# Weight sums in earlier slots, a shorter wait for one low part, three banks for the down products

## The reference

```
def ffn(x, w_gate, w_up, w_down):          # w_gate, w_up 512 x 2048, w_down 2048 x 512
    h = silu(x @ w_gate) * (x @ w_up)
    g = h.reshape(B, S, 2048 // 4, 4)
    _, idx = top_k(abs(g), 2)              # keep 2 of every 4
    return (g * mask(idx)).reshape(h.shape) @ w_down
x = x + layernorm(attn(layernorm(x)))
x = x + layernorm(ffn(layernorm(x)))
```

## Time and profile before

| | |
|---|---|
| median of 3 runs | 1237.51 us (1236.67 to 1240.82) |
| profiled execution, its own time | 1238.83 us |
| its span in the trace | 1237.0 us |
| mean granted TensorE clock | 0.978 |
| PE busy | 1180.2 us (95%), 5862 matmul records |
| DVE busy | 861.3 us (70%) |
| ACT / POOL busy | 520.7 us (42%) / 504.2 us (41%) |
| DMA | 153.78 MB, mean 124 GB/s |

### The profile page before, as it was taken

The page is one execution under the profiler, slowest core; times in us unless marked ns, Lnnn a source line. Parts: engine busy times, 40 slices in busy tenths (PEclk is TensorE's granted clock), DMA queues, the critical chain, the costliest instruction groups (busy, mean ns, idle before and its releaser), DMA issues.

```text
span 1237.0 us, 16282 instructions
## 1 busy us (share of the span) xinstructions
PE 1180.2 (95%) x5862; PEld 989.3 (80%) x5862; DVE 861.3 (70%) x1416; ACT 520.7 (42%) x1017; POOL 504.2 (41%) x393
## 2 busy tenths in 40 slices
PE   8999999999999999999999899996997899999986
PEld 7888888888888888888888677784885678888865
DVE  8945666666755556666665897967779469768698
ACT  5534535545454345453455333324423244334332
POOL 6422424424644144252455654554523542112124
PEclk9999999999999999999999899996999899999998
DMA  6321423314443233142356467682523555343421
GB/s 217 87 71 43 112 61 89 95 31 119 116 130 90 69 87 95 43 116 52 97 153 204 151 223 249 222 292 79 190 69 102 164 191 181 120 153 119 153 68 69
DMA packets 96368, 153.78 MB, mean 124 GB/s; under 512 B 10272, under 2 KB 31008, under 8 KB 96288
## 3 DMA queue, kind: packets, MB, share of 16 engines
q1 hardware_dynamic: 96288, 152.74, 39.4%
HBM read 96.60 MB, written 40.89 MB: 111 GB/s over the span
## 4 chain that ended last, share of the span: by engine, by line
PE 77%; DVE 13%; DMA 3%; ACT 2%; issue 2%; POOL 2%; SPq 2%; DVEq 0%; ACTq 0%; POOLq 0%
PE bank_q L784 8%; PE bank_q L786 8%; PE bank_q L785 8%; PE bank_y L786 5%; PE bank_y L785 5%; PE bank_y L784 5%; PE bank_od L1011 5%; PE bank_od L1014 4%; PE bank_t L784 3%; PE bank_t L786 3%; PE bank_t L785 3%; PE bank_s L908 2%; PE bank_od L784 2%; PE bank_od L785 2%; PE bank_od L786 2%; PE bank_s L784 2%
## 5 line engine op out<-in xcount | busy, mean ns | idle before, releaser
L784 PE MATMUL bank_q<-x_hi,w_hi 128*128 128x512 f32 x464 | 187.6, 404 | 13.7 <-POOL x_lo L1910 11.6
L786 PE MATMUL bank_q<-x_lo,w_hi 128*128 128x512 f32 x464 | 182.4, 393 | 0.0
L785 PE MATMUL bank_q<-x_hi,w_lo 128*128 128x512 f32 x464 | 182.1, 392 | 0.0
L1910 POOL TENSOR_TENSOR w_lo<-stage,w_hi 128x512 fp32r<-128x512 f32 x60 | 80.5, 1352 | 114.0 <-ACT w_hi L1190 113.2
L1910 POOL TENSOR_TENSOR big_lo<-q_rows,big_hi 128x1024 fp32r<-128x1024 f32 x31 | 73.9, 2385 | 117.1 <-ACT big_hi L1229 117.1
L784 PEld LDWEIGHTS bank_q<-x_hi,w_hi 128*128 128x128 f32 x464 | 88.1, 190 | 31.2 <-POOL x_lo L1910 12.0
L786 PEld LDWEIGHTS bank_q<-x_lo,w_hi 128*128 128x128 f32 x464 | 87.9, 189 | 19.2
L785 PEld LDWEIGHTS bank_q<-x_hi,w_lo 128*128 128x128 f32 x464 | 88.2, 190 | 16.8
L786 PE MATMUL bank_y<-wout_lo,a_hi 128*128 128x512 f32 x256 | 100.0, 391 | 0.0
L785 PE MATMUL bank_y<-wout_hi,a_lo 128*128 128x512 f32 x256 | 99.8, 390 | 0.0
L784 PE MATMUL bank_y<-wout_hi,a_hi 128*128 128x512 f32 x256 | 99.8, 390 | 0.0
(11 more groups left out here) (421 smaller groups left out, 3104.3 us busy)
## 6 DMA issues: line engine op xcount, KB each, us to landing
q_rows<-scratch SPq DMA_DIRECT2D x116, 128.0 KB, 2.3
x_rows<-x SPq DMA_DIRECT2D x48, 256.0 KB, 3.0
stage<-wq SPq DMA_DIRECT2D x32, 256.0 KB, 2.7
stage<-wo SPq DMA_DIRECT2D x32, 256.0 KB, 2.7
s_keep<-x_hi SPq DMA_DIRECT2D x16, 512.0 KB, 4.4
s_keep<-x_lo SPq DMA_DIRECT2D x16, 512.0 KB, 5.3
w_hi<-s_keep SPq DMA_DIRECT2D x32, 256.0 KB, 3.1
w_lo<-s_keep SPq DMA_DIRECT2D x32, 256.0 KB, 3.7
```

The source lines that it names most:

```text
L784: pe.matmul(ps, whi, xhi, start=first, stop=False, skip_group_check=True)
L785: pe.matmul(ps, wlo, xhi, start=False, stop=False, skip_group_check=True)
L786: return pe.matmul(ps, whi, xlo, start=False, stop=last, skip_group_check=True)
L1910: return pool.tensor_tensor(dst, full, hi.bitcast(F32), ALU.subtract)
```

## The change

Seven edits:

1. `t_low(2)`: POOL waits for step 7 of the row sums (counter 8) where it waited for step 8 (counter 9).
2. `SUM_AT`: the 16 rounds are summed in slots 1 to 15, four to a group, where they ran to slot 20, three to a group. A load then stands at most one slot ahead of its sum from round 8 on.
3. Down products of the first block go round three banks (psO, psD, psY) instead of two; the turns (`mid, 1`) all use bank psSt; the addition of a down product is written before the choice.
4. The low part of the last down piece of a unit, made by DVE (L1494), is made by POOL behind the hidden lows; counter dve_wl is gone.
5. DVE's lows of rows 2 and 3 (`first_lows`) come behind the hidden product of the next slot.
6. Down products 29, 30 and 31 are made in slots 36, 38, 40 (before 35, 36, 37); loads and splits of the next unit's last pieces move with them, and `ld_d` has eight semaphores instead of four.
7. Down product 50 is made in slot 64 (before: 61), as one of six; its addition stands between `pair_1` and `keep_masks`, that of 51 between masks and rows.

```diff
-        return y + 6
+        return y + 6 if y < EDGE - 3 else (36, 38, 40)[y - EDGE + 3]
     if y >= LAST:
         return y + 9
-    return SLOTS if y > 50 else 8 * (y // 8) + 11 + min(y % 8, 6)
+    return SLOTS if y > 49 else 8 * (y // 8) + 11 + min(y % 8, 6)
...
+def down_place(y):
+    if y < EDGE:
+        return y % 3
+    return y % 4 if y < SLOTS - 4 else 4 + y % 4
...
-SUM_AT = [1, 2, 3, 5, 6, 7, 9, 10, 11, 13, 14, 15, 17, 18, 19, 20]
+SUM_AT = [1, 2, 2, 3, 5, 6, 6, 7, 9, 10, 10, 11, 13, 14, 14, 15]
...
-DOWN_LD = {NU: (33, 33, 33, 39), NU + 1: (39, 39, 39, 39), NU + 2: (51, 51, 51, 51), NU + 3: (59, 59, 59, 59)}
-DOWN_AT = {NU: (35, 36, 37, 41), NU + 1: (42, 43, 44, 45), NU + 2: (52, 53, 54, 55), NU + 3: (60, 61, 62, 63)}
+DOWN_LD = {NU: (33, 33, 33, 41), NU + 1: (41, 41, 41, 41), NU + 2: (51, 51, 51, 51), NU + 3: (59, 59, 59, 59)}
+DOWN_AT = {NU: (35, 36, 37, 42), NU + 1: (43, 44, 45, 46), NU + 2: (52, 53, 54, 55), NU + 3: (60, 61, 62, 63)}
...
-        psX = [psY, psSt]
+        psX = [psSt, psSt]
...
         def down_bank(y):
-            if y < EDGE:
-                return (psO, psD)[y % 2]
-            if y < SLOTS - 4:
-                return (psO, psD, psY[:, :], psS[:, :])[y % 4]
-            return (gX, uX, gY, uY)[y % 4]
+            return (psO, psD, psY[:, :], psS[:, :], gX, uX, gY, uY)[down_place(y)]
...
-                if y < EDGE + 2:
-                    g.wait_ge(dve_yf, y - 1)
+                g.wait_ge(dve_y, SLOTS)
+                g.wait_ge(dve_yf, same_place(y) + 1)
...
-            def split(k):
-                hi, lo = dest(PLAN[k][0])
-                g.wait_ge(act_wh, k + 1)
-                dve.tensor_tensor(lo, stage[:, k % RING_W, :], hi.bitcast(F32), ALU.subtract).then_inc(dve_wl, 1)
...
+            def first_lows(d):
                 for i in range(2, 4):
                     g.wait_ge(act_hh, 4 * d + i + 1)
                     dve.tensor_tensor(hidden(d)[1][:, i, :], hid[:, i, :], hidden(d)[0][:, i, :].bitcast(F32),
...
-                    keep_two(n // 4 - 1)
                 if n < EDGE:
                     for y in downs:
                         add_down(y)
+                if n % 4 == 0 and 4 <= n <= EDGE:
+                    keep_two(n // 4 - 1)
+                if n == EDGE:
+                    first_lows(n // 4 - 1)
+                if n % 4 == 1 and 4 < n < EDGE:
+                    first_lows(n // 4 - 1)
...
                     keep_masks(NU - 1, 0)
+                    add_down(downs[1])
                     keep_rows(NU - 1, 0)
                     hidden_lows(NU - 1, 0)
-                    for y in downs[1:]:
+                    for y in downs[2:]:
                         add_down(y)
...
-                to, of, count = ((T1, raw_t1, 7), (T3, raw_t3, 6), (T2, raw_t2, 9), (T4, raw_t4, 10))[n]
+                to, of, count = ((T1, raw_t1, 7), (T3, raw_t3, 6), (T2, raw_t2, 8), (T4, raw_t4, 10))[n]
```

More of the change, by code:

```diff
@@ L64, in add_beat, with same_place @@
     return n if n >= SLOTS or n < EDGE else n + 1
+def down_place(y):
+    if y < EDGE:
+        return y % 3
+    return y % 4 if y < SLOTS - 4 else 4 + y % 4
+def same_place(y):
+    return max([i for i in range(y) if down_place(i) == down_place(y)], default=-1)
 def downs_at(n):
@@ L214, with last_down @@
 PIECE = {piece: k for k, (piece, _) in enumerate(PLAN)}
-def by_dve(piece):
+def last_down(piece):
     return piece[0] == "d" and piece[2] == 3
-def split_count(k):
-    kind = by_dve(PLAN[k][0])
-    return sum(by_dve(piece) == kind for piece, _ in PLAN[:k + 1])
 def pieces_at(tick, kinds):
@@ L480, in build @@
         st_k = [sem(f"st_k{i}") for i in range(8)]
-        ld_d = [sem(f"ld_d{i}") for i in range(4)]
+        ld_d = [sem(f"ld_d{i}") for i in range(8)]
         act_d, pool_d = sem("act_d"), sem("pool_d")
@@ L511, in split_wait @@
             k = PIECE[piece]
-            gate.wait_ge(dve_wl if by_dve(piece) else pool_wl, split_count(k))
+            gate.wait_ge(pool_wl, k + 1)
         def halves(kind, b, t):
@@ L556, in load_piece @@
                     before = k - RING_W
[L557 removed]
+                    g.wait_ge(pool_wl, before + 1)
                 sp.dma_start(stage[:, k % RING_W, :], src).then_inc(ld_w[k % RING_W], 16)
@@ L1340, in slot_f @@
                 for k in pieces_at(tick, "d"):
-                    if not by_dve(PLAN[k][0]):
+                    if not last_down(PLAN[k][0]):
                         split(k)
@@ L1662, in combine_x @@
                 if step == 6:
-                    g.wait_ge(pool_wl, split_count(max(k for k in range(len(PLAN)) if not by_dve(PLAN[k][0]))))
-                    g.wait_ge(dve_wl, NU)
+                    g.wait_ge(pool_wl, len(PLAN))
                 g.wait_ge(dve_t, (0, 0, 1, 2, 3, 4, 5, 7, 8, 9)[step])
@@ L1839, in slot_f @@
                     variance(job)
-                for k in pieces_at(tick, "d"):
-                    if by_dve(PLAN[k][0]):
-                        split(k)
                 for r in range(ROUNDS):
@@ L1994, in slot_f @@
                         lo(hidden(d)[1][:, i, :], hid[:, i, :], hidden(d)[0][:, i, :]).then_inc(pool_hl, 1)
-                for k in pieces_at(tick, "gu"):
+                for k in pieces_at(tick, "gud"):
+                    if not last_down(PLAN[k][0]) and PLAN[k][0][0] == "d":
+                        continue
                     split(k)
```

20 lines of the change are left out of this document (8 added, 12 removed).

## The result

The changed kernel takes 1245.46 us (median of 6 runs, 1242.56 to 1248.78); the kernel before, run beside it, 1237.97 (6 runs, 1236.67 to 1240.82). The ratio is 1.006, with a 95% interval of 1.004 to 1.0079: slower by about 7.5 us where 20 us of gain were forecast. The profiled execution took 1244.29 us.

What follows compares the result with a forecast made beforehand. DVE with SP's queue was taken to bound slots 6 to 16, PE afterwards except single stops. −15 + 20 + 11.4 + 3.5 + 0 = 19.9 us gain, giving 1217.5 us by the median; range 1201 to 1233.

Steps and rivals of the forecast that it cites:

- the early loss: Slots 1 to 16: four rounds a group make slot 16 15 us later, bounds 3 and 33.
- the mark: End of slot 16's up product on PE: near 810 (before, 797.1); before 801 or after 820 refutes the largest term.
- The waits: DVE in slots 5, 9, 13 and 14: late loads cost 30 us of waits against 11.1, 19 more.
- The work: DVE, slots 1 to 16: four more sums at 2.5 us, 10 us, less 8.5 for three splits of 2.85.
- The 7 us taken off for slack: Slots 1 to 16: DVE lateness PE doesn't see, through the addition before the choice, a third bank and later lows.
- The mechanism: Slots 5 to 16: DVE's waits for x_part grow from 11 to between 25 and 35 us.
- the rival of the other side: Slots 1 to 16: sums' loads in SP's queue become the bound, groups cost up to 45 us; 1240 to 1252, chance 0.08.
- Slots 16 to 32: Stop from ACT's wait for the last store goes: 12.0 us, clock 6, fewer sums 2; gain 20, bounds 8 and 24.
- the slot itself: Turns in one bank: one a slot (8.2 us), reading under 2, so cost 0; if it fails, up to 2.0 a turn.
- T2's low part: PE's 11.6 us wait for POOL near 960 goes, clock gives 1.8, next lateness costs 2: gain 11.4.
- Edits 6 and 7: Slots 36 to 40: gain 3.5, bounds 0 and 5; end of kernel: product only moves, 0, bounds −3 and +3.
- The rule of the Trainium skill: Splits moved to POOL still block DVE by the shared port: 8.5 us shrink to about 4, sum 4 us worse.

Runs made afterwards that it cites:

- t2_loads_first: Kernel before with edit 1, loads of the sums issued ahead of their slot's weight pieces on SP, old table of slots: 1226.17 us, ratio 0.9895.
- edit 4 alone: Kernel before with edit 1 and edit 4 (last down piece of a unit split by POOL): 1228.60 us, against 1225.86 with edit 1 only.
- loads_first: Changed kernel with each round's load (from round 4 on) issued on SP ahead of its slot's weight pieces: 1231.39 us, ratio 0.9947 to the kernel before.
- three_turns: Kernel before with edits 1, 5, 6 and the eight turns one slot later (slots 20 to 27): 1212.42 us, ratio 0.9798.
- old_slots_banks: Changed kernel with the old table of slots and the old two banks for down products and turns: 1229.11 us, ratio 0.993 to the kernel before.
- only_slots: Kernel before with edit 2's table of slots alone: 1260.38 us, ratio 1.0182.
- thin_slots: Kernel before with edit 2's table of slots, DVE's sums of weights done on 16 of 256 columns: 1252.01 us, ratio 1.0111.
- thin_old: Kernel before, old table of slots, DVE's sums of weights done on 16 of 256 columns: 1231.83 us, ratio 0.9947 (three executions).

## Why the prediction was wrong

*What bounds the kernel* was read rightly for the changed kernel: in slots 1 to 16 DVE sets the pace, and it waits for loads. For the kernel before, the 11.1 us of waits that the prediction put into the bound were worth nothing (t2_loads_first): without them DVE's operations took longer instead.

*The step that failed is the early loss* ("DVE is late by 10 + 19 − 8.5 = 20.5 us ... I take these 7 off ... 15 us later at slot 16"). It was 32.8 on DVE, and 28.8 on PE at the mark, so outside the 801 to 820 that the prediction allowed for its largest term. Three terms of it were off, each by about as much as the others:
- The waits. 19 us more were forecast, 24.9 came. The three places were sized well as a sum (9, 12 and 9 against 9.8, 12.7 and 7.1 us), but each of the first two groups had a second round whose load is late behind the first: 2.9 us in slot 6 and 4.8 in slot 10, which the sum left out. Another 1.7 us came from waits that the sum had not looked at: 3.8 for POOL's hidden lows, which edit 5 puts behind the next hidden product, less 2.1 for a cast.
- The work. 10 − 8.5 = 1.5 us were forecast, 7.1 came. The sums cost 3.3 us each in the trace of the kernel before (39.3 us for 12) and 3.4 after (54.1 for 16), where the prediction took 2.5: 14.8 us in place of 10. The splits that DVE no longer makes were not three of 2.85 us. Up to slot 16 there are two, and only one of them is long:

```profile
L1494 DVE TENSOR_TENSOR wout_lo<-stage,wout_hi 128x512 fp32r<-128x512 f32 x2 | 3.7, 1837 | 2.1 <-ACT wout_hi L1190 2.1
```

So 3.7 us in place of 8.5. The other operations of DVE took about 4 us less together. On POOL the splits were not free either: edit 4 alone gave a median 2.7 us higher.
- The 7 us taken off for slack. The same text had shown that DVE waits only 0.2 us for PE in this stretch, so there is little that could make up for a late DVE. On PE 4 us of them seem to be there at the end of slot 16, and 1.2 two slots later (31.6 against 32.8). Nor can edit 5 be called for them: what it gives doesn't show in slots 1 to 16. PE's waits changed their name, from y_acc to the hidden product.

By DVE's account the forecast's 15 us are to be raised by 5.9 and 1.7 for waits, 5.6 for work and 7 for the slack; the 1.5 us for a lower clock have no place in it, and 0.8 us go for the earlier start: 32.9, against 32.8 measured. The granted clock did fall in the stretch, from 0.95 to 0.87, but DVE waits for PE only 0.5 us there, so it can't have made DVE late by much.

The mechanism was the predicted one, down to the place and the single wait; its size was the upper bound of the range given for it (33), where that bound had the three groups alone: they lost 10.5, 12.7 and 7.0 us, and slots 1 to 4 another 3.4. The time itself, 1245.46 us, lies in the range of the rival of the other side (1240 to 1252, chance 0.08), which wanted an early loss of 35 us or more and groups of up to 45 us; the first two took 46.0 and 48.2. Its picture, a load behind a store behind the sum of a load that is late itself, is what the second rounds of slots 6 and 10 and the 20.0 us left in loads_first show. That rival deserved more than 0.08.

*Slots 16 to 32*: 14.9 us for the 20 forecast. The chain from the stores to ACT went as a whole, as said. PE's idle time in the stretch fell by 7.3 us (12.7 to 5.4) where 12.0 were forecast; slot 32 began at 959.4 in place of 937. What came new are 2.4 us at a turn's single bank, and stops of 0.8 and 0.7 us for lows. Edit 3, costed at 0 with "the slot itself" as cover, costs 4.7 us on top of three_turns, with one wait of 7.05 us: the cover was a slot of PE, but the reader of the bank is DVE, and its queue is taken by the choice and by sums for longer. In the changed kernel no sums are made in slot 20, and the wait is 2.4 us.

*T2's low part*: forecast 11.4, measured 11.7 alone; in the changed kernel PE has no wait for POOL's x_lo left between 940 and 990, as said. *Edits 6 and 7*: behind slot 32 the changed kernel gained 12.4 us against the 14.9 of these terms together. Edit 6 was put at 3.5 and gave about 1.7. For edit 7, put at 0, no run stands alone; in the trace the wait of 5.3 us at the end is 3.1, and one of 2.9 us for the sum of a gate product (L1711) has come, so by the trace it hardly moves anything, as said; no experiment shows it.

The rule of the Trainium skill that was weighed (the page "SBUF — State Buffer", section "SBUF: two separate sides": DVE with two SBUF inputs and GpSimd block each other) spoke for a smaller gain of edit 4. The runs go further in the same direction, a median 2.7 us higher; that it is the port and not POOL's queue is not shown by them. In the changed kernel a DVE operation of a sum still takes as long as its POOL neighbour:

```profile
719.74 2.60 DVE L1643 TENSOR_TENSOR x_part<-x_part 128x256 f32<-128x256 f32 x1
722.27 0.41 DVE L1645 TENSOR_TENSOR x_part<-x_part 128x256 f32<-128x256 f32 x1
```
```profile
719.50 2.57 POOL L1906 TENSOR_TENSOR x_lo<-x_part,x_hi 128x1024 fp32r<-128x1024 f32 x1
```

2.60 us beside POOL's 2.57, and 0.41 for the next one alone.

What stays open: the parts, each measured on another base, add up to 14.1 us of loss (−11.7, +22.8, +2.7, −2.7, −1.7 and +4.7 for edits 1, 2, 4, 5, 6 and 3; by way of old_slots_banks −11.7 + 3.2 + 22.8 = 14.3), where the change measured 7.5. Three banks take the place of waits for y_acc that the new table makes long (14.5 us in only_slots), so edit 3 may be worth something there; that was not tried apart. Between loads_first and the changed kernel only the order of SP's issues differs, so 14 us of the loss stand on the loads' place however the rest is shared out.

## What to carry to other kernels

When the profile says that an engine sets the pace of a stretch, count what delays it nearly in full: here 31.6 of DVE's 32.8 us reached PE. But a wait that is taken away is not yet time won. Twice a part of it came back as longer operations of the same engine, so look at busy time and waits together. A load whose buffer is freed by a store in the same in-order queue can't be asked for earlier by asking for its use earlier; look at what stands ahead of it in the queue, and give it a place ahead of the issues that block. And where two things collide, price both sides of the collision: moving eight turns by one slot won 7.7 us by removing the same stop for which sixteen rounds of sums were moved, at a net cost of 22.8.

## What the runs showed of the hardware

An operation of DVE beside one of POOL can last as long as POOL's, and this doesn't hang on its own size. In thin_slots a sum of 128x16, which takes 0.17 us alone, took 2.43 beside a POOL operation of 2.4 (two in 4.76):

```profile
726.56 2.43 DVE L1649 TENSOR_TENSOR x_part<-x_part 128x16 f32<-128x16 f32 x1
```
```profile
726.55 4.76 POOL L1910 TENSOR_TENSOR x_lo<-x_part,x_hi 128x1024 fp32r<-128x1024 f32 x2
```

So the time that such a collision costs did not shrink with DVE's work here. It also depends on the moment at which DVE comes: where the loads came earlier, DVE's waits fell by 10.1 us and its busy time rose by 8.0 (t2_loads_first), and by 19.8 and 6.7 (loads_first). That all of this rise is POOL's doing is a reading of such rows, not the result of an experiment.

One issue at the head of SP's queue that waited for a split on POOL kept all later ones back for 16.3 us (732.56 to 748.82); putting the loads of the sums ahead of such pieces was worth 14 us (loads_first).

One execution of thin_old took 4206.39 us. Its trace shows where the time went: PE is busy for 4189.5 of 4204.6 us, a 128x512 matmul takes its turn every 0.84 us where the other traces have 0.23 (0.43 at the lower clock), and DVE is busy no longer than usual (814.9 us). The granted clock in its rows is 1.00, so the clock shown doesn't explain it, and nothing in the study says what does.

```profile
2499.91 1.15 PE L784 MATMUL bank_od<-wout_hi,big_hi 128*128 128x512 f32 x1
2500.75 1.15 PE L785 MATMUL bank_od<-wout_hi,big_lo 128*128 128x512 f32 x1
```
